# Stage 1 of a three-stage transformer block in another order: paired gram bursts, transposes between the projections, h normalized with one factor

## The reference, cut to what matters

```
x  = x + 0.5 * ffn(layernorm(x))            # the small net: 512 -> 64 -> (x16, relu, sum) -> 64 -> 512
y  = layernorm(x)                           # eps 1e-5
h  = rmsnorm(y, ln1_scale)                  # eps 1e-6; y * rsqrt(mean(y^2) + eps) * ln1_scale
q, k, v = h @ wq + bq, h @ wk + bk, h @ wv + bv;   k = k / (|k| + 1e-6);   beta = sigmoid(h @ wbeta + bbeta)
# 16 heads of 32, token by token:  S += beta * (v - S k) k^T;   o = S q
y  = y + o @ wo + bo
y  = y + gelu(rmsnorm(y, ln2_scale) @ w1 + b1) @ w2 + b2
x  = x + y
x  = x + 0.5 * ffn(layernorm(x))
```

## Time and profile before

| | |
|---|---|
| median of 3 runs | 3609.17 us (3599.86 to 3610.68) |
| the profiled execution | 3609.92 us, its span 3608.1 us |
| mean granted TensorE clock | 0.97 |
| stage 1, to stage 2's first DMAs | about 0 to 1099.6 us |
| tiles 1 to 13 of stage 1 | 832.6 us, 13 x 64.05 |
| stage 1's TensorE line of one tile without a system | 61.8 us (tile 8) |

### The profile page before, as it was taken

The page is one execution under the profiler, slowest core; times in us unless marked ns, Lnnn a source line. Parts: engine busy times, 40 slices in busy tenths (PEclk is TensorE's granted clock), DMA queues, the critical chain, the costliest instruction groups (busy, mean ns, idle before and its releaser), DMA issues. The chain is left out here.

```text
span 3608.1 us, 150299 instructions
## 1 busy us (share of the span) xinstructions
PE 3335.6 (92%) x68430; PEld 2614.6 (72%) x68430; DVE 1865.4 (52%) x3036; ACT 1325.0 (37%) x2630; POOL 1151.6 (32%) x1207
## 2 busy tenths in 40 slices
PE   3999999899986999999995999999999999999997
PEld 2766666666665788888884877777777777777775
DVE  4767777677765878777713233333323333333323
ACT  3444444344421333333334333333333333333332
POOL 0334545354543655555511011212211211212210
PEclk7999999999997999999997999999999999999998
DMA  3254443545446566666554011110010011110010
GB/s 92 83 155 134 141 141 118 153 130 147 124 141 189 184 193 200 190 193 193 173 179 154 1 36 36 36 36 25 23 36 32 27 36 36 35 36 24 24 36 24
DMA packets 388099, 355.43 MB, mean 99 GB/s; under 512 B 58128, under 2 KB 320912, under 8 KB 384912
## 3 DMA queue, kind: packets, MB, share of 16 engines
q1 hardware_dynamic: 385632, 351.27, 31.3%
q10 hardware_dynamic: 2224, 0.90, 0.1%
HBM read 184.19 MB, written 153.09 MB: 93 GB/s over the span
## 5 line engine op out<-in xcount | busy, mean ns | idle before, releaser
L1778 DVE TENSOR_TENSOR glo<-gl,gh 128x512 fp32r<-128x512 f32 x256 | 195.3, 763 | 925.6 <-ACT gh L1685 925.5
L1681 ACT ACTIVATE gl<-bank,b1m 128x512 f32<-128x512 f32 x256 | 175.9, 687 | 796.2 <-PE bank L232 796.2
L230 PE MATMUL bank<-w_hi,gh 128*128 128x512 f32 x1024 | 410.3, 401 | 24.7 <-DVE glo L1778 24.7
L230 PE MATMUL bank<-h_hi,w_hi 128*128 128x512 f32 x1024 | 425.5, 416 | 4.0 <-DVE w_lo L1822 4.0
L232 PE MATMUL bank<-w_hi,glo 128*128 128x512 f32 x1024 | 406.6, 397 | 0.0
L232 PE MATMUL bank<-h_hi,w_lo 128*128 128x512 f32 x1024 | 406.4, 397 | 0.0
L231 PE MATMUL bank<-h_lo,w_hi 128*128 128x512 f32 x1024 | 405.9, 396 | 0.0
L231 PE MATMUL bank<-w_lo,gh 128*128 128x512 f32 x1024 | 405.5, 396 | 0.0
L230 PEld LDWEIGHTS bank<-w_hi,gh 128*128 128x128 f32 x1024 | 193.0, 188 | 75.6 <-DVE glo L1778 31.7
L1183 PE MATMUL bank<-ringA 32*32 32x32 f32 x16512 | 238.9, 196 | 7.8 <-issue 5.0
L964 POOL TENSOR_TENSOR nrm<-nrm,cst 128x16 f32<-128x16 f32 x64 | 190.0, 2969 | 153.7 <-DVE nrm L738 153.4
(11 more groups left out here) (172 smaller groups left out, 7149.5 us busy)
## 6 DMA issues: line engine op xcount, KB each, us to landing
ringB<-heads_scratch SPq DMA_DIRECT2D x256, 192.0 KB, 2.7
ringA<-heads_scratch SPq DMA_DIRECT2D x258, 128.0 KB, 2.2
X<-in_L_attn_x SPq DMA_DIRECT2D x16, 1024.0 KB, 9.7
x_scratch<-X SPq DMA_DIRECT2D x16, 1024.0 KB, 5.4
heads_scratch<-vb SPq DMA_DIRECT2D x16, 1024.0 KB, 11.5
heads_scratch<-qk SPq DMA_DIRECT2D x16, 1024.0 KB, 10.6
heads_scratch<-kb SPq DMA_DIRECT2D x16, 1024.0 KB, 5.2
heads_scratch<-kbuf SPq DMA_DIRECT2D x16, 1024.0 KB, 8.5
```

The lines of the kernel that those rows point to most:

```text
L230: e.matmul(o, lhs[0], rhs[0], start=first, stop=False)
L1681: e.activation(gl[k][:, :], bank[k][:, :], ACT.Gelu_apprx_tanh, bias=b1m[:, m:m + 1]).then_inc(a_gl, 1)
L1778: e.tensor_tensor(gh[k][1][:, :], gl[k][:, :], gh[k][0][:, :], ALU.subtract).then_inc(v_gl, 1)
```

## The change

All engines get a new order for a tile, kept consistent with each other, and h gets one factor instead of two.

- TensorE: gram bursts go in pairs: (4, 5) of tile t-1 behind projection 3, (6, 7) behind projection 7; (0, 1) of tile t behind projection 9, (2, 3) at the end of tile t. x turns 0, 1 stand behind projection 9, x turns 2, 3 behind 10, h turns 0 to 2 behind 11, h turn 3 behind the last projection (12). The next tile's projections come right behind bursts 2, 3. `TURNS` is gone.
- Banks: x turns use 3, 4, 3, 4; h turns 3, 4, 5, and h turn 3 uses the bank of projection 11 (`h_bank`).
- h: ScalarE's `norm1` applies the product of both norms at once, with the scale `sc1` = ((1 + 1e-6) var + 1e-11)^-0.5 and the shift `sh1` = -mean * `sc1`. `scale_h`, `ri` and `inverse` are gone; `nm_x1` and `rs_x1`, which stage 2 reads, are made separately (`shift_x1`, `deviation_x1`).
- SyncE issues the system's store ahead of x1's.
- The waits of `x_turned` on the system buffers are split: on the way in for turn 0, on the way out for turn 2.

```diff
-H_BANK, X_BANK, WIN_BANK = (3, 4, 3, 5), (5, 4, 3, 4), 5
-
-TURNS = (("h", 0), ("h", 1), ("x", 0), ("g", 0), ("h", 2), ("x", 1), ("h", 3), ("g", 1), ("x", 2), ("x", 3))
+H_BANK, X_BANK, WIN_BANK = (3, 4, 5), (3, 4, 3, 4), 5
...
+        def h_bank(t, f):
+
+            return H_BANK[f] if f < 3 else (13 * t - 2) % 3
...
+                store_system0(t)
                 if t + 1 < NT:
                     store_x1(t + 1)
-                store_system0(t)
...
# pe_project, the loop over tiles
-                for g4 in range(1, GROUPS):
-                    if t:
-                        gram(t - 1, 2 * g4)
-                    project(t, 3 * g4 + 1)
-                    if t:
-                        gram(t - 1, 2 * g4 + 1)
-                    project(t, 3 * g4 + 2)
-                    project(t, 3 * g4 + 3)
-                    if g4 == 1 and t + 1 < NT:
-                        ffn_out(t + 1)
-                for what, n in TURNS:
...
+                if t:
+                    gram(t - 1, 4)
+                    gram(t - 1, 5)
+                project(t, 4)
+                project(t, 5)
+                project(t, 6)
+                if t + 1 < NT:
+                    ffn_out(t + 1)
+                project(t, 7)
+                if t:
+                    gram(t - 1, 6)
+                    gram(t - 1, 7)
+                project(t, 8)
+                project(t, 9)
+                if t + 2 < NT:
+                    turn_x(t + 2, 0)
+                    turn_x(t + 2, 1)
+                gram(t, 0)
+                gram(t, 1)
+                project(t, 10)
+                if t + 2 < NT:
+                    turn_x(t + 2, 2)
+                    turn_x(t + 2, 3)
+                project(t, 11)
+                if t + 1 < NT:
+                    for f in range(3):
+                        turn_h(t + 1, f)
+                project(t, 12)
+                if t + 1 < NT:
+                    turn_h(t + 1, 3)
+                gram(t, 2)
+                gram(t, 3)
...
# act_project: norm1
-                e.activation(Y[i][:, b, :], X[i][:, b, :], ACT.Identity, bias=nm_x1[:, NB * t + b:NB * t + b + 1],
-                             scale=rs_x1[:, NB * t + b:NB * t + b + 1]).then_inc(a_y1, 1)
+                e.activation(Y[i][:, b, :], X[i][:, b, :], ACT.Identity, bias=sh1[:, b:b + 1],
+                             scale=sc1[:, b:b + 1]).then_inc(a_y1, 1)
...
# act_project, end of a tile
                 evict(t, 11)
+                if nxt:
+                    for f in range(NF):
+                        h_turned(t + 1, f)
                 evict(t, 12)
...
# dve_project
             def shift1(t):
-
+                e.wait_ge(o_rs1, 4 * t + 2)
+                e.scalar_tensor_tensor(sh1[:, :], mv1[1][:, :, 0], -1.0, sc1[:, :],
+                                       ALU.mult, ALU.mult).then_inc(v_nm1, 1)
+
+            def shift_x1(t):
                 u = slice(NB * t, NB * t + NB)
-                e.wait_ge(o_rs1, 2 * t + 2)
+                e.wait_ge(o_rs1, 4 * t + 4)
...
-            def scale_h(t, b):
-                e.wait_ge(a_y1, 4 * t + b + 1)
-                if b == 0:
-                    e.wait_ge(o_ri, t + 1)
-                e.tensor_scalar(Y[t % 2][:, b, :], Y[t % 2][:, b, :], ri[:, b:b + 1], None,
-                                ALU.mult).then_inc(v_h, 1)
...
# pool_project
             def deviation1(t):
+
+                e.wait_ge(v_ag1, t + 1)
+                if t:
+                    e.wait_ge(a_y1, 4 * t)
+                e.tensor_scalar(sc1[:, :], mv1[1][:, :, 1], 1.0 + RMS_EPS, RMS_EPS * LN_EPS,
+                                ALU.mult, ALU.add).then_inc(o_rs1, 1)
+                e.wait_ge(o_rs1, 4 * t + 1)
+                e.tensor_tensor(sc1[:, :], sc1[:, :], neg_half, ALU.pow).then_inc(o_rs1, 1)
+
+            def deviation_x1(t):
...
-            def inverse(t):
-                e.wait_ge(v_ri, 3 * t + 3)
-                e.tensor_tensor(ri[:, :], ri[:, :], neg_half, ALU.pow).then_inc(o_ri, 1)
...
                 root(t, 0)
-                beta_k(t, 0)
+                system0(t, 2)
                 if t + 1 < NT:
                     deviation1(t + 1)
+                beta_k(t, 0)
                 root(t, 1)
                 if t + 1 < NT:
-                    inverse(t + 1)
+                    deviation_x1(t + 1)
                 beta_k(t, 1)
-                system0(t, 2)
                 root(t, 2)
                 system0(t, 3)
```

More of the change, by code:

```diff
@@ L421, in pe_project @@
                 project(t, 3)
-                for g4 in range(1, GROUPS):
-                    if t:
-                        gram(t - 1, 2 * g4)
-                    project(t, 3 * g4 + 1)
-                    if t:
-                        gram(t - 1, 2 * g4 + 1)
-                    project(t, 3 * g4 + 2)
-                    project(t, 3 * g4 + 3)
-                    if g4 == 1 and t + 1 < NT:
-                        ffn_out(t + 1)
-                for what, n in TURNS:
[L433 to L439, removed]
+                if t:
[30 more added lines that the diff above has]
+                gram(t, 3)
+            for n in range(4, NG):
                 gram(NT - 1, n)
@@ L839, in dve_project @@
             for t in range(NT):
+                nxt, nx2 = t + 1 < NT, t + 2 < NT
+                if t:
+                    mask(t - 1, 2)
+                    mask(t - 1, 3)
+                    turn_k(t - 1, 3)
                 turn_beta(t)
@@ L852, in dve_project @@
                     turn_kb(t - 1, 2)
-                if t + 2 < NT:
+                if nx2:
+                    stats0(t + 2, 0)
+                    stats0(t + 2, 1)
+                if nxt:
+                    sums(t + 1, 2, 3)
+                if nx2:
                     stats0(t + 2, 2)
@@ L883, in dve_project @@
[L883 removed]
+                turn_k(t, 1)
+                if nxt:
                     add_ffn(t + 1)
[L885 to L898 removed]
@@ L910, in dve_project @@
-                scale_k(t, 1)
-                if t:
-                    mask(t - 1, 7)
-                if t + 1 < NT:
-                    scale_h(t + 1, 2)
-                    scale_h(t + 1, 3)
-                norms(t, 2)
-                turn_kb(t, 1)
-                turn_k(t, 3)
-                for what, n in TURNS:
-                    if what == "g":
-                        mask(t, n)
-                    elif what == "h" and t + 1 < NT:
-                        h_low(t + 1, n)
+                    mask(t - 1, 7)
@@ new lines, in dve_project @@
+                if nxt:
+                    shift1(t + 1)
+                turn_kb(t, 0)
+                if nx2:
+                    for b in range(NB):
+                        add_bout(t + 2, b)
+                turn_k(t, 2)
+                scale_k(t, 1)
+                norms(t, 2)
+                turn_v(t, 3)
+                turn_kb(t, 1)
+                if nxt:
+                    shift_x1(t + 1)
+                mask(t, 0)
+                mask(t, 1)
+                if nxt:
+                    for f in range(NF):
+                        h_low(t + 1, f)
@@ L924, in dve_project @@
+            mask(NT - 1, 2)
+            mask(NT - 1, 3)
+            turn_k(NT - 1, 3)
             scale_k(NT - 1, 2)
@@ L927, in dve_project @@
             scale_k(NT - 1, 3)
-            for n in range(2, 6):
-                mask(NT - 1, n)
+            mask(NT - 1, 4)
+            mask(NT - 1, 5)
             turn_kb(NT - 1, 3)
-            for n in range(6, NG):
-                mask(NT - 1, n)
+            mask(NT - 1, 6)
+            mask(NT - 1, 7)
         def pool_project(e):
```

155 lines of the change are left out of this document (59 added, 96 removed).

## The result

The changed kernel takes 3514.99 us (median of 4 runs, 3511.48 to 3519.07), the kernel before 3609.81 (4 runs, 3599.86 to 3610.68): ratio 0.9744, 95% interval 0.9724 to 0.9764. That is 95 us less.

The account below looks back on a forecast made before the run. Bound: TensorE, busy 92% of the span, plus its waits for VectorE and half clock. Terms -27 - 14 + 0 + 2 - 1 - 12 - 4 - 5 = -61 take 3609.9 to 3549 us; range 3532 to 3592.

Parts of the forecast that it names:

- End of tile: From the last projection to the next tile's first: TensorE's idle for hT_lo goes, -27 us (bounds -27 and 0).
- The walk of VectorE: VectorE's steps timed from S, a tile's first projection matmul: last sums end S+25.1, TensorE wants g at S+25.6, no wait.
- B: Rival: VectorE late at the last sums, 2 us a tile, +28 us, 3577; chance 0.22.
- D: Rival, slower: the wait for pb moves to mask 0, ahead of gram 2; at 5 us 3619; chance 0.08.
- Systems: Tiles 6, 9, 12, with 1024-wide transposes at the last sums: TensorE's 3.10 us wait becomes about 3.6, +2 us in all.
- Tail: Behind the last projection, up to stage 2: the last power starts 1.7 us earlier, -5 us (bounds -1, -8).
- Rival C: The clock falls more often: one more half-speed projection a tile, +32 us, 3581; chance 0.09.
- TensorE's own work: Count of TensorE's instructions in a tile: moved transposes and bursts cost the same elsewhere; 58.5 to 59 us a tile.
- the pairing: A second gram burst directly behind a first: costed at 0, bounds -6 to +9 us over 13 tiles with four pairs.
- FFN output: Third output matmul's wait for the first add: 1.0 of 1.67 us idle goes, -14 in 14 tiles (bounds 0, -18).
- the clock's -12: Half clock in tiles 1 to 13: half of up to 25 us lost work comes back, -12 (bounds 0, -22).
- One factor: Scalings and a third power for h go, off the path; before the loop two scalings leave the chain, -1 us.

Follow-up runs that it names:

- e1: The kernel before, with VectorE making all four hT_lo ahead of masks 0 and 1 of the tile: 3595.15 us, ratio 0.9947.
- e4: The changed kernel, with all eight turns (x, then h) in one run behind projection 12, ahead of bursts 2 and 3: 3562.65 us, ratio 0.9862.
- e9: The kernel before, with h by one factor alone, the order of all the rest kept: 3585.80 us, ratio 0.9923.
- three_parts: The kernel before with the edits of e1, e3 and e9 together, TensorE's order untouched: 3553.00 us, ratio 0.9825.
- e12: The kernel of three_parts, with the four x turns moved from the tile's end to behind projections 9 and 10: 3548.97 us, ratio 0.9820.
- e10: The changed kernel, with bursts 2 and 3 at each tile's end issued twice over: 3625.83 us, ratio 1.0037.
- e3: The kernel before, with three of VectorE's bias adds moved from ahead of the FFN adds to behind them: 3591.43 us, ratio 0.9937.

## Why the prediction was wrong

**Right, step by step.** *End of tile*: hT_lo's wait is gone, -27.3 as taken, and so is the wait for pb, while its landing is unchanged. That all of it came depends on VectorE's new order up to the sums: in e1, with the old one, 16.4 of it moved to g. The walk of VectorE held: last sums forecast at S+25.1, measured S+25.5 (384.53 - 359.08); masks 6 and 7 done S+38.5 against S+37.9; mask 0 at S+49.6 against S+48.4 (407.51). That decides the rivals: B needed the sums late by 2 us in plain tiles, D the mask, and neither was. B's place is the thin one all the same: the tiles behind a system's (4, 7, 10, 13) wait 0.7 us for g. *Systems*: +2 forecast, the wait for g rose from 11.6 to 13.9. That the size fits is in part luck: the systems' tiles give 0.9 of it (10.2 to 11.1), the plain tiles the other 1.4. *Tail*: -5 forecast, 33.1 to 27.9; the last power starts 7.6 us behind projection 12's end (980.2), where the earlier trace rows has 9.3, the 1.7 that was forecast:

```profile
987.79 2.89 POOL L968 TENSOR_TENSOR nrm<-nrm,cst 128x16 f32<-128x16 f32 x1 [0.24 <-DVE nrm L750]
```

*Rival C*, more half clock: it went from 40.9 to 10.2 us in the middle tiles. The three stretches left, at 445.1, 619.2 and 793.3, each follow the 3 us wait for g in a system's tile; none begins at the transposes mid-tile, and putting these back to the end (e4) more than doubled the half-clock time. The Trainium skill ("TensorE: Matmul & The Clock Gate", Part 4: PE-mode transpose) says that the clock's upper level doesn't engage for them, as they don't count as busy in the same way; that they would cool three more places by this rule was not seen.

**The step that failed** is the one on TensorE's own work: "The transposes and bursts that moved are paid elsewhere at the same price", with the pairing at 0 and the idle that the waits view doesn't name left at "some 10 us are other". It took the middle tiles' busy time, clock apart, as constant, and that fell by 21 us (35.9 less 15 of clock). The forecast's own count of a tile's work shows it too: its terms add up to 58.35 us (it wrote 58.5 to 59), and plain tiles from 5 on took 56.3 to 57.3. A turn was priced at 0.5, from the 1.09 of two; the next instruction starts 0.93 behind these two (at 630.77), and in the new order a turn costs 0.44. By term, forecast against measured:

| term | forecast | measured |
|---|---|---|
| hT_lo's wait | -27 | -27.3 |
| FFN output | -14 in 14 tiles | -21.1 in 13: wait -12.3, and -8.8 in the matmuls |
| stalls inside bursts | not counted | -8.8 |
| work of bursts | 0 | -8.4, of it 6.8 for pairs (52 x 0.13) |
| turns | 0 | -9.1 |
| systems, wait for g | +2 | +2.3 |
| first projections at half clock | in the clock's -12 | -8.7 |
| tiles 0, 14, 15 and ahead of the loop | -5 | about -6 |
| tail | -5 | -5 |
| later stages | 0 | about -3, within the noise (2502.2 to 2509.8 in all traces) |

What was missed is in four rows: stalls 8.8, bursts 8.4, turns 9.1, output 7; with 3 in the later stages and 3 less than taken in the clock's row this is the whole 34 us (-61 against -95). They overlap with the clock: 30.7 us less at half clock is 15 us of work regained, against 12 taken, 8.7 of it in the beta projections and the other 6 in the rows of output, bursts and turns. So the clock's size was nearly right. Of the 34, some 18 are bursts, turns and output that took less time at full clock than the forecast gave them, and 9 are stalls. All of these have the same sign, which is why the sum fell out of the range. It gave bounds to the pairing alone (-6 to +9, where its own 0.9 against 1.03 makes -6.8 for 52 pairs, and -6.8 is what came), and none to the others.

Two attributions failed as well. One factor was costed at -1, for VectorE off the path; alone it gives 28 (e9), mostly because it shortens the same wait for pb that the new order removes: 11 of hT_lo's idle and some 9 of clock, and 4 ahead of tile 1. In the full change the two overlap. And what three_parts leaves is not the x turns' place by itself (4 us, e12): undone in the changed kernel, with the h turns, the turns' place costs 48 (e4). A similar edit, four turns moved in one and seven in the other, is worth 4 us where VectorE is late and 48 where it isn't.

**What stays open.** The -3.4 of the turns between e12 and the changed kernel, and the share of the output's matmuls, were read in traces and not run alone. That TensorE waits for its instructions in the stalls rests on their timing (97 of 97 end 2.2 to 2.6 us after a load starts) and on the growth with the number of short instructions (e10), not on an experiment on the load itself, and the same is true of the late loads: that they wait for the data transfers ahead of them is read from 18 coincidences, not from a run with those transfers moved. What brings half-clock time isn't settled either: it followed long waits and stalls most often, but not the sum of the idle (e1, e3).

## What to carry to other kernels

Look at how long a run of short instructions an engine must get through at once, and split it with long ones: with all transposes ahead of the bursts at a tile's end the same instructions cost 48 us more, about half of it in stalls. An engine that is idle a quarter of the time can still set the time through the DMA that it releases; price an edit by which store or bank it brings forward, not by the engine's busy share. And where several terms of a sum are set to "same as before", give each a bound and ask whether they all point the same way.

## What the hardware showed that was not expected

TensorE stopped inside runs of short matmuls with no semaphore to wait for: 4 times by 2.0 to 2.3 us in the kernel before (160 transposes and small matmuls in a run), never inside a burst of tiles 1 to 14 of the changed one or of e12 (runs of at most 136 and 144; the changed kernel has one stop of 1.6 us in its tail, where six bursts stand in a row), 6 times by up to 3.8 with 32 transposes ahead of a pair (e4), 12 times by up to 4.4 with 256 matmuls in a row (e10). Each of these stops ends 2.2 to 2.6 us after a 16 KB load of instructions starts (434.0 to 436.2 in e4, 188.2 to 190.4 before), though the load's own packet takes only about 1 us (0.97 in both). In the 18 stalls over 2.5 us (e4, e10) the load started only as the data transfers ran out, up to 2.1 us after TensorE had stopped. The Trainium skill ("Runtime: NRT & Kernel Launch", Instruction fetch mechanics) says that an engine's instructions come in blocks of 16 KiB, the next fetched while the current one runs, at a cost that is mostly hidden. The size agrees with the trace, 16384 bytes a load; in runs of instructions this short the cost wasn't hidden here. What follows such a gap often runs at the clock's lower level, 1.2 GHz, for 3.4 or 6.8 us (all four times before, twice of four in three_parts), so a stall can cost more than its length. Switching from a projection to a burst and back costs about 0.13 us, no more.
